# One piece a group for probabilities times values, and six steps moved to groups 1 and 2, in a two-layer attention and memory kernel

## What is computed

```
xn = layernorm(x)
s  = causal attention over xn: 16 heads of 8 features, softmax, probabilities times values
g  = silu(top-2 mixture of 8 experts over xn)
x  = x + s * g
xn = layernorm(x)
s  = xn + y      # y: a linear memory W, updated token by token from keys, values and queries of layernorm(xn)
g  = silu(xn @ sign(weight).T)
x  = x + s * g
```

## Time and profile before

| what | us |
|---|---|
| median of 3 runs | 621.88 (619.85 to 626.63) |
| the profiled execution | 621.56 |
| its span, first to last instruction | 619.8 |
| PE busy | 578.6 (93%) |
| DVE busy | 391.4 (63%) |
| ACT busy | 353.0 (57%) |
| POOL busy | 171.3 (28%) |

### The profile page before, as it was taken

One profiled execution on the slowest core, in us unless ns is written; L12 is line 12 of the kernel. 1 busy time (PEld: TensorE's weight loads), 2 busy tenths in 40 slices (PEclk: granted clock), 3 DMA queues, 4 the chain that ended last, 5 costly groups with the idle time before them and its releaser, 6 DMA issues.

```text
span 619.8 us, 17493 instructions
## 1 busy us (share of the span) xinstructions
PE 578.6 (93%) x7289; PEld 387.4 (62%) x7289; DVE 391.4 (63%) x975; ACT 353.0 (57%) x679; POOL 171.3 (28%) x335
## 2 busy tenths in 40 slices
...
GB/s 118 157 155 126 26 96 87 165 59 65 63 116 75 24 20 122 96 44 2 66 129 74 12 28 114 96 43 4 78 112 70 2 12 1 24 20 2 3 3 35
DMA packets 58163, 39.42 MB, mean 64 GB/s; under 512 B 17957, under 2 KB 57988, under 8 KB 58084
## 3 DMA queue, kind: packets, MB, share of 16 engines
...
## 4 chain that ended last, share of the span: by engine, by line
PE 70%; DVE 16%; issue 5%; ACT 5%; POOL 3%; DMA 1%; SPq 0%; DVEq 0%; POOLq 0%
PE ps_v L950 10%; PE ps_s L930 9%; PE ps_a L865 5%; DVE cand L1458 5%; PE ps_e L911 5%; PE ps_a L851 4%; PE ps_c L1015 3%; PE ps_e L738 3%; PE ps_a L820 3%; PE ps_e L903 2%; PE ps_e L907 2%; PE ps_s L933 2%; PE ps_c L997 2%; PE ps_c L1100 2%; DVE stats L1378 2%
## 5 line engine op out<-in xcount | busy, mean ns | idle before, releaser
L1458 DVE TENSOR_REDUCE cand<-ps_s 128x4 f32<-128x512 f32 (+1 forms) x320 | 212.6, 685 | 63.5 <-PE ps_s L933 44.3
L1252 ACT ACTIVATE prob<-ps_e 128x512 f32<-128x512 f32 x320 | 188.8, 599 | 89.6 <-PE ps_e L911 53.9
L930 PE MATMUL ps_s<-kst,qst 72*128 72x128 bf16 (+2 forms) x1024 | 125.1, 234 | 12.5 <-DVE cand L1458 9.1
L930 PEld LDWEIGHTS ps_s<-kst,qst 72*128 72x128 bf16 (+1 forms) x1024 | 72.0, 98 | 72.3 <-DVE cand L1458 38.9
L911 PE MATMUL ps_e<-qst,kst 75*128 75x256 bf16 (+3 forms) x416 | 104.6, 282 | 0.0
L950 PE MATMUL ps_v<-prob,vaug 128*32 128x512 f32 (+3 forms) x1024 | 89.0, 444 | 0.0
L903 PE MATMUL ps_e<-identb,negmask 128*128 128x150 bf16 (+3 forms) x320 | 72.7, 227 | 8.6 <-ACT prob L1252 8.5
L907 PE MATMUL ps_e<-qst,kst 128*128 128x128 bf16 x384 | 74.4, 220 | 0.0
L911 PEld LDWEIGHTS ps_e<-qst,kst 75*128 75x128 bf16 x416 | 40.6, 98 | 3.5
L903 PEld LDWEIGHTS ps_e<-identb,negmask 128*128 128x128 bf16 x320 | 31.2, 97 | 18.4 <-ACT prob L1252 14.2
L738 PE MATMUL ps_e<-identb 128*128 128x512 bf16 x115 | 40.0, 402 | 1.9 <-POOL identb L520 1.9
...
## 6 DMA issues: line engine op xcount, KB each, us to landing
...
```

The lines of the kernel that those rows point to most:

```text
L930: last = mm(ps_s[:, bank, w * n:w * (n + 1)], q[0:rows, hd, tok(i)], k[0:rows, hd, keys[0]:keys[1]], start=(n == 0), stop=True, skip_group ...
L1252: af(prob[:, u, :], ps_e[:, u % 2, :], ACT.Exp).then_inc(S["e_emptied"], 1)
L1458: vec.tensor_reduce(cand[:, i, h0:h0 + FILLS * (len(hds) - 1) + 1:FILLS, S_SLOT[u]], ps_s[:, u % 2, :].rearrange("p (a c) -> p a c", a=len ...
```

## The change

Four things change.
- **One piece.** In `PLAN` the three pieces become one step `pv` (512, 384, 128 and 256 columns in a row) at (1, 2), (2, 2), (3, 2) and, for group 3, in the seam at (4, 1), now behind `v` and `c_y2`. `prob` grows from 10 to 14 slots: units 0 to 3 of odd groups have four of their own. `pv_used` counts once a group. `LAST_PLAN` keeps the three pieces.
- **The gate.** `gb1`, `gb2`, `gb3` go from group 0 to (1, 1), (1, 4), (1, 6), `out` from (1, 1) to (1, 8), and `gt` from (1, 8) to (2, 3).
- **The second layer.** `xn2_norm` goes from (0, 7) to (1, 6), `c_xn2t` from (1, 0) to (1, 9) and from the bank `ps_c0` to `ps_c1`, and `c_ffn` from (1, 4) to (2, 1). POOL's `rn` and `c_out` wait for other semaphores, since `xn2_norm` is later.
- **The seam.** `v` comes before `pv`, and `c_r3` before `yt`.

```diff
+SLOTS = 14
...
-C0_PIECES = ("c_xn2t", "c_kt", "c_vk", "c_gram", "lev_a1", "lev_a2", "lev_a3", "lev_a4", "lev_a5", "lev_a6",
+C0_PIECES = ("c_kt", "c_vk", "c_gram", "lev_a1", "lev_a2", "lev_a3", "lev_a4", "lev_a5", "lev_a6",
...
-C1_PIECES = ("c_ht", "c_qt", "c_vk", "c_gram", "c_ffn", "lev_d5", "lev_d6", "c_y3")
+C1_PIECES = ("c_ht", "c_qt", "c_vk", "c_gram", "c_xn2t", "c_ffn", "lev_d5", "lev_d6", "c_y3")
...
-    (3, 9): ["pv1", "c_u2"], (4, 0): ["m_parts1", "gelu", "stacks1"], (4, 1): ["pv2", "c_y2"], (4, 2): ["v"], (4, 3): ["yt", "x1", "c_r3"],
+    (3, 9): ["c_u2"], (4, 0): ["m_parts1", "gelu", "stacks1"], (4, 1): ["v", "c_y2", "pv"], (4, 3): ["c_r3", "yt", "x1"],
...
-        prob = sb("prob", [P, UNITS, 512])
+        prob = sb("prob", [P, SLOTS, 512])
...
+        def slot(grp, u):
+
+            return u if u >= HEADS // GROUPS or grp % 2 == 0 else UNITS + u
...
-                after(pool, S["norm1"], NT * (b.c - 1))
+                after(pool, S["norm2"], NT * (b.c - 1))
...
-                    pool.wait_ge(S["norm1"], NT * (b.c + 2))
+                    pool.wait_ge(r.S["c0_emptied"], C0_NUMBER[b.c + 1, "c_kt"] + 1)
...
-            def pv(b, grp, piece):
-
-                if piece == 0:
+            def pv(b, grp, pieces):
+
+                if 0 in pieces:
...
-                pe.wait_ge(S["e_emptied"], b.count(GROUPS * UNITS, UNITS * grp + (4, 8, 10)[piece]))
-                for j, u0, at in (((0, 0, 0),), ((1, 4, 0), (3, 4, 384)), ((2, 8, 0),))[piece]:
+                pe.wait_ge(S["e_emptied"], b.count(GROUPS * UNITS, UNITS * grp + (4, 8, 10)[pieces[-1]]))
+                for j, u0, at in sum((((((0, 0, 0),), ((1, 4, 0), (3, 4, 384)), ((2, 8, 0),))[piece]) for piece in pieces), ()):
...
-                                  prob[:, u, o:o + TOK - P * j], start=(j == 0 and grp % FILLS == 0),
+                                  prob[:, slot(grp, u), o:o + TOK - P * j], start=(j == 0 and grp % FILLS == 0),
...
-                last.then_inc(S["pv_used"], 1)
+                if 2 in pieces:
+                    last.then_inc(S["pv_used"], 1)
...
-                c0_fill(b, "c_xn2t")
+                c1_fill(b, "c_xn2t")
...
-                pe.wait_ge(r.S["c0_emptied"], C0_NUMBER[b.c, "c_xn2t"] + 1)
...
-                after(act, S["pv_used"], b.count(3 * GROUPS, 0))
+                after(act, S["pv_used"], b.count(GROUPS, 0))
...
-                if u in (0, 4, 8):
-                    after(act, S["pv_used"], cur.count(3 * GROUPS, 3 * (grp - 1) + u // 4 + 1))
-                af(prob[:, u, :], ps_e[:, u % 2, :], ACT.Exp).then_inc(S["e_emptied"], 1)
+                if u in (0, 4):
+                    after(act, S["pv_used"], cur.count(GROUPS, grp - 1 + u // 4))
+                af(prob[:, slot(grp, u), :], ps_e[:, u % 2, :], ACT.Exp).then_inc(S["e_emptied"], 1)
```

More of the change, by code:

```diff
@@ L53 @@
 A_PIECES = ("xnt", "q", "k", "logits", "gt", "m_rows0", "h0", "h1", "h2", "h3", "v", "gb0", "gb1", "gb2", "gb3", "m_rows1", "out")
-C0_PIECES = ("c_xn2t", "c_kt", "c_vk", "c_gram", "lev_a1", "lev_a2", "lev_a3", "lev_a4", "lev_a5", "lev_a6",
+C0_PIECES = ("c_kt", "c_vk", "c_gram", "lev_a1", "lev_a2", "lev_a3", "lev_a4", "lev_a5", "lev_a6",
              "lev_d1", "lev_d2", "lev_d3", "lev_d4", "lev_d5", "c_u0", "c_u1", "c_u2", "c_u3", "c_r1", "c_r2", "c_r3", "c_y0", "c_y1", "c_y2")
-C1_PIECES = ("c_ht", "c_qt", "c_vk", "c_gram", "c_ffn", "lev_d5", "lev_d6", "c_y3")
+C1_PIECES = ("c_ht", "c_qt", "c_vk", "c_gram", "c_xn2t", "c_ffn", "lev_d5", "lev_d6", "c_y3")
 PLAN = {
-    (0, 0): ["c_u3"], (0, 1): ["gb0"], (0, 2): ["ln2_stats", "c_y3"], (0, 4): ["gb1", "ln2_rstd", "hn_norm"],
-    (0, 6): ["pv0", "gb2"], (0, 7): ["c_ht", "xn2_norm", "rn", "c_out"], (0, 8): ["gb3"], (0, 9): ["pv1", "c_kt", "c_qt"],
-    (1, 0): ["load_x", "m_rows1", "c_xn2t"], (1, 1): ["c_vk", "out"], (1, 2): ["c_gram", "pv2"], (1, 3): ["logits"],
[6 rows of a table removed]
+    (0, 0): ["c_u3"], (0, 1): ["gb0"], (0, 2): ["ln2_stats", "c_y3"], (0, 4): ["ln2_rstd", "hn_norm"],
+    (0, 7): ["c_ht", "rn", "c_out"], (0, 9): ["c_kt", "c_qt"],
+    (1, 0): ["load_x", "m_rows1"], (1, 1): ["c_vk", "gb1"], (1, 2): ["c_gram", "pv"], (1, 3): ["logits"],
[6 rows of a table added]
 }
@@ L99 @@
 PLAN_OLDER = ("c_u3", "c_y3", "c_out")
-PLAN_CURRENT = ("gb0", "gb1", "gb2", "gb3", "out", "pv0", "pv1", "pv2", "yt", "x1", "m_rows1", "zero_state")
+PLAN_CURRENT = ("gb0", "gb1", "gb2", "gb3", "out", "pv0", "pv1", "pv2", "pv", "yt", "x1", "m_rows1", "zero_state")
 SEQUENCES = 8
@@ L159, in iteration @@
                 if of is not None:
-                    yield name, (of, step) if name in ("pv0", "pv1") else (of, step - 1) if name in ("pv2", "yt") else (of,)
+                    yield name, (of, step) if name in ("pv0", "pv1") else (of, step - 1) if name in ("pv", "pv2", "yt") else (of,)
 def schedule():
@@ L1118, in _ @@
             pieces = {"xnt": xnt, "q": lambda b: qk(b, 0), "k": lambda b: qk(b, 1), "v": v, "logits": logits, "gt": gt,
-                      "out": out_piece, "m_rows0": lambda b: m_rows(b, 0), "m_rows1": lambda b: m_rows(b, 1), "pv0": lambda b, grp: pv(b, grp, 0), "pv1": lambda b, grp: pv(b, grp, 1), "pv2": lambda b, grp: pv(b, grp, 2), "yt": yt, "c_xn2t": c_xn2t, "c_ht": c_ht, "c_kt": c_kt,
+                      "out": out_piece, "m_rows0": lambda b: m_rows(b, 0), "m_rows1": lambda b: m_rows(b, 1), "pv": lambda b, grp: pv(b, grp, (0, 1, 2)), "pv0": lambda b, grp: pv(b, grp, (0,)), "pv1": lambda b, grp: pv(b, grp, (1,)), "pv2": lambda b, grp: pv(b, grp, (2,)), "yt": yt, "c_xn2t": c_xn2t, "c_ht": c_ht, "c_kt": c_kt,
                       "c_qt": c_qt, "c_vk": c_vk, "c_gram": c_gram, "c_ffn": c_ffn}
@@ L1261, in c_xn2t @@
                 r, o = second_layer(b)
-                c0_full(b, "c_xn2t")
-                copy(r.xn2T[:, :], r.ps_c0[:, :]).then_inc(r.S["c0_emptied"], 1)
+                c1_full(b, "c_xn2t")
+                copy(r.xn2T[:, :], r.ps_c1[:, :]).then_inc(r.S["c1_emptied"], 1)
             def c_ht(b):
```

12 lines of the change are left out of this document (6 added, 6 removed), and 14 rows, old and new, of tables (LAST_PLAN, PLAN).

## The result

The changed kernel takes 640.79 us (median of 4 runs, 638.71 to 642.63) against 620.87 of the kernel before (619.75 to 626.63): ratio 1.0314, 95% interval 1.0274 to 1.0353. It is 20 us slower, outside the range of the prediction. The profiled execution, at 638.71 us the fastest of its four, has a span of 637.0 us, before 619.8.

The account below looks back on a forecast made before the run. PE, busy 93%, sets the pace, except in group 0, where DVE is busy 12.98 of 14.07 us. Five iterations +7.2, first −3, seventh +0.6, last sequence −2: sum +2.8 on 621.56, so 624 us, range 610 to 634.

Parts of the forecast that it names:

- the clock: Rival: idle PE in group 0 drops the clock each iteration, 5 to 6 times 1.3 us more, 631 us; chance 0.21.
- first iteration with a `cur`: No second layer: group 0 −2.2, group 1 by 0.6 and group 2 by 1.1 shorter, seam gives back 0.8; about −3.
- last sequence: At its start most of PE's 1.63 us wait for ACT goes, perhaps the half-clock stretch too: −2 us.
- seam: From (3, 6) to group 0: `pv0` leaves, joined piece comes, `c_r3` leaves 0.44 us of waiting; +0.25 us.
- group 0: DVE sets its 14.07 us; a multiplication leaves DVE's chain, `gb3` and `pv1` leave PE: −1.65 us.
- group 1: Joined `pv` and three multiplications come; two pieces, `c_ffn`, `gt` and 0.85 us idle go; 1.1 wait at `out`: −0.6 us.
- group 2 to `lev_a6`: Joined `pv` and `c_ffn` come; removed pieces worth 2.18 us return only 0.8, as they covered a chain: +1.75 us.
- from `lev_a6` on: Joined `pv` at (3, 2), where nothing waits before or after: +1.70 us.
- The saving of a join: A whole group costs PE 2.84 us in three pieces and 2.36 in one, 0.48 less.
- The point of decision: The idle stretch on PE from which the clock falls: about 1.6 us.
- PE stays the bound: Rival: all overheads come back, no new wait forms, −1.9 us in seven iterations, 608 us; chance 0.22.
- The block starves ACT and DVE: Rival: during `pv` ACT and DVE run short of units, four places cost 1.5 us more, 633 us; chance 0.12.

Follow-up runs that it names:

- run 1: The changed kernel plus matmuls that compute nothing in group 0 (eight behind unit 4, four behind unit 6): 626.91 us, ratio 1.0117 to the kernel before.
- run 12: The changed kernel with the seam's steps back in the old order, nothing else undone: 637.19 us, ratio 1.0254 to the kernel before.
- run 8: The moves alone, three pieces a group, but the seam in the changed kernel's order: 617.26 us, ratio 0.9943 to the kernel before.
- run 4: The changed kernel with groups 0 and 2 back in three pieces, groups 1 and 3 joined, new seam: 624.25 us, ratio 1.0074 to the kernel before.
- run 3: The changed kernel with three pieces in every group and the old seam, so the moves alone: 611.76 us, ratio 0.9857 to the kernel before.
- run 5: The kernel before with only gate multiplications 1 to 3 and `out` at their new places: 630.10 us, ratio 1.0165 to the kernel before.
- run 11: The moves alone with only group 0's pieces joined, behind unit 2 of group 1, old seam: 617.24 us, ratio 0.9921 to the kernel before.

## Why the prediction was wrong

Its direction was undecided (0.33 for slower), its time and range were too low by 17 and 7 us. The step that failed is the clock: its falls stood beside the sum, as a rival, and not in it. The parts of the sum, against the difference of the two profiled executions:

| part | predicted | measured |
|---|---|---|
| five iterations with all parts, at full clock | +7.2 | +4.6 |
| first iteration with a `cur`, less its fall | −3 | +0.7 |
| seventh iteration, at full clock | +0.6 | +0.4 |
| last sequence | −2 | +0.2 |
| preparation | 0 | −0.1 |
| seven falls in the iterations | 0 | +11.4 |
| sum | +2.8 | +17.2 |

"At full clock" is read from run 1. The changed kernel's second to seventh iterations are together 9.9 us longer than those of run 1, which is the price of six falls. The first iteration's fall is 1.5 us: run 12, which has none there, takes 17.37 us for that group 1, the changed kernel 18.87. By the medians the difference is 19.9 us, as the profiled execution is the fastest of the changed kernel. Point by point, by the prediction's own steps.

**The stretches of the iteration were right within 0.3 us each.** Without the clock (run 1 for group 0, the changed kernel for the rest):

| stretch | predicted | measured |
|---|---|---|
| seam | +0.25 | +0.04 |
| group 0 | −1.65 | −1.66 |
| group 1 | −0.6 | −0.88 |
| group 2 to `lev_a6` | +1.75 | +1.71 |
| from `lev_a6` on | +1.70 | +1.71 |
| sum | +1.45 | +0.92 |

The details hold too: `x1`'s wait 0.34 on DVE (0.3), 2.11 and 0.94 on PE before units 5 and 7 (2.2 and 1.1), 0.95 before `lev_a6` (0.85), no long wait at the start of the last sequence. In group 1 the waits came to 0.76 for 1.1, and at the units before `out` instead of at `out`. The other term that was off is the seam's, where `c_r3` left 0.17 of waiting and not 0.44. The saving of a join, 0.48 us, was a little high: runs 8 and 4 differ in group 3 by its join alone, with the same waits behind it, and by 0.40. But the saving counts only in such a place. In the other groups two pieces are worth about 2 us of PE, and their removal gave back 0.99, 1.00 and 0.77, while the joined piece cost 1.71 to 1.73 each time (predicted 1.70). The prediction also says that the rows show the cost of a change of mode on both sides of a piece; its rows show 0.10 us on entry and nothing of the exit.

**The clock was the failed step.** It was called a rival with 0.21, for idle stretches that the forecast itself counted on. Its mechanism is shown by run 1: the falls go when PE has something to do in group 0, and 12 of the 20 us with them, and they stay in the one iteration without filler. Its price for a fall was nearly right, 1.3 predicted, 71.67 − 70.20 = 1.47 measured. Wrong were two things. It was given as an alternative to the forecast, though both rest on the same 2.2 us (measured 2.11). And it counted "5 to 6 times" one short fall, where the profile has eight falls behind the preparation, two of them 6.8 us long, the first already in group 1 of the first iteration with a `cur` (78.8 us). The last of the eight, at the last sequence, the kernel before has too. The point of decision, "about 1.6 us", is half right: 2.10 us alone gave four falls in ten iterations, and 1.03 us as the longest stretch one in fifteen (runs 3, 5 and 11).

The Trainium skill (TensorE: Matmul & The Clock Gate, HAM oscillation) describes a kernel in which TensorE waits about 3 to 5 us for a DMA in every round, goes cold each time and pays for it in every round. The trace of the changed kernel agrees that a wait that recurs can bring a fall each time, six in six iterations, and it shows this for a wait for DVE of 2.11 us, shorter than those of that kernel.

**The ends were wrong by sign.** They stood in the sum with −3 for the first iteration with a `cur`, and −2 for the last sequence's. The first took 56.38 us for 54.14, one fall of 1.5 in it: +0.7. Group 0 fell by 2.8 (predicted 2.2), but "its group 1 by 0.6" failed: that number holds the departure of `c_ffn` and the idle 0.85, neither of which exists in this iteration; the prediction's own terms without them give +1.2, and run 12, without a fall there, measured +1.7. Group 2 gave 0.15 and not 1.1. And the seam does not give back 0.8: without a `c_r3` nothing covers the copy of `yT`, and PE waits 0.81 us.

At the last sequence the wait of 1.63 us is gone as foreseen, and yet nothing is gained: from its first unit to the end it takes 92.38 us, before 92.23. The waits of PE over the last 100 us, changed kernel, then before:

```profile
PE ps_e L908 <- ACT prob L1257: 2.4, 6, 0.7
PE ps_a L863 <- DVE hid L1447: 2.1, 2, 1.1
```

```profile
PE ps_e L903 <- ACT prob L1252: 3.8, 7, 1.6
...
PE ps_a L858 <- DVE hid L1442: 0.2, 1, 0.2
```

1.4 us less for ACT, 1.9 more for DVE and its multiplications by the gates. That later statistics hold these up is likely, since in run 12, with the old seam, that row is 1.0, but it is not shown. The fall there stayed as well (553.2 us for 532.0). Run 12 has none there and takes 90.50 us, so most of the −2 would have come only if the fall had gone too.

**The other rivals.** "PE stays the bound" fell: by the rule of the drain (the Trainium skill, TensorEngine Tiling (Array Packing), Key Properties) a change of tiling mode drains TensorE. Runs 3 and 11 agree as far as group 0's join takes 0.22 us from PE's busy time; but in groups 0 to 2 the time saved is not on the path. "The block starves ACT and DVE" is not seen: what waits there is in group 1, 0.28 and 0.48 us, and it is within the forecast's 1.1.

**Where the gain was.** Not expected at all: the moves without the join give 1.78 us an iteration (run 3). Group 0 is 0.92 us shorter, group 1 is 1.61 shorter, and group 2 is 0.75 longer. Run 5 shows that group 0's part comes with the gates' move alone; the rest is not taken apart. With three pieces a group 611.76 us, 1.4% under the kernel before.
